# A non-local block in f32: theta and phi by plain f32 matmuls of 64 columns on two column tiles, theta's stack filled by transfers

## The reference

```python
theta = einsum('bhwc,cd->bhwd', x, W_theta)             # 32 channels, 1024 pixels
phi   = maxpool2x2(einsum('bhwc,cd->bhwd', x, W_phi))   # 32 channels, 256 cells
g     = maxpool2x2(einsum('bhwc,cd->bhwd', x, W_g))     # 128 channels, 256 cells
beta  = softmax(einsum('bqd,bkd->bqk', theta, phi), axis=-1)
tmp   = einsum('bqk,bkv->bqv', beta, g)
out   = gamma * einsum('bhwv,vc->bhwc', tmp, W_o) + x
```

## Time and profile before

| | |
|---|---|
| median of 2 runs | 240.32 us (240.01 and 240.63) |
| span of the profiled execution, first to last instruction | 237.7 us; the page gives no other time of its own for it |
| median less that span | 2.6 us |
| PE busy | 232.0 us, 98% |
| DVE busy | 205.3 us, 86% |
| POOL, ACT busy | 167.3 us (70%), 147.8 us (62%) |
| granted TensorE clock | 0.999 of full |
| moved by transfers | 51.14 MB, 215 GB/s |
| chain that ended last | PE 89%, DMA 5%, DVE 4% |

### The profile page before, as it was taken

The page is one execution under the profiler, slowest core; times in us unless marked ns, Lnnn a source line. Parts: engine busy times, 40 slices in busy tenths (PEclk is TensorE's granted clock), DMA queues, the critical chain, the costliest instruction groups (busy, mean ns, idle before and its releaser), DMA issues.

```text
span 237.7 us, 4361 instructions
## 1 busy us (share of the span) xinstructions
PE 232.0 (98%) x1464; PEld 207.8 (87%) x1464; DVE 205.3 (86%) x475; ACT 147.8 (62%) x274; POOL 167.3 (70%) x119
## 2 busy tenths in 40 slices
PE   7999999999999999999999999999999999999994
PEld 4777888988989899898989989898998989989794
DVE  5699988989888898988989899898988989899785
ACT  3665948577483866838477492847748385645640
POOL 1488698868679686768867677786867868642870
PEclk9999999999999999999999999999999999999999
DMA  7693029396592937739194683928659293725854
GB/s 238 220 365 128 3 70 337 130 272 258 119 374 88 337 151 242 292 105 382 60 327 191 194 341 108 343 85 289 241 150 383 61 338 139 247 107 190 318 204 181
DMA packets 14934, 51.14 MB, mean 215 GB/s; under 512 B 1856, under 2 KB 2496, under 8 KB 14912
## 3 DMA queue, kind: packets, MB, share of 16 engines
q1 hardware_dynamic: 14512, 50.67, 60.6%
q10 hardware_dynamic: 400, 0.20, 0.3%
HBM read 33.95 MB, written 16.78 MB: 213 GB/s over the span
## 4 chain that ended last, share of the span: by engine, by line
PE 89%; DMA 5%; DVE 4%; issue 1%; ACT 1%; SPq 0%; DVEq 0%
PE proj L209 23%; PE out L350 18%; PE proj L216 12%; PE proj L350 8%; PE score L255 6%; PE shift L350 6%; PE shift L310 5%; PE score L350 4%; PE score L282 4%; DMA x_t<-in_xt 2%; DMA out<-y_sb 2%; PE shift L209 1%; DVE y_sb L669 1%; DVE neg_parts L643 1%; PE score L265 1%; PE out L282 1%
## 5 line engine op out<-in xcount | busy, mean ns | idle before, releaser
L564 POOL TENSOR_TENSOR e_lo<-e_sb,e_hi 128x512 fp32r<-128x512 f32 x64 | 82.0, 1294 | 45.7 <-ACT e_sb L488 45.7
L559 POOL TENSOR_TENSOR x_lo<-x_t,x_hi 128x1024 fp32r<-128x1024 f32 x30 | 71.8, 2399 | 8.7 <-ACT x_hi L444 8.7
L485 ACT ACTIVATE e_hi<-shift 128x512 fp32r<-128x512 f32 x60 | 36.0, 600 | 17.9 <-PE shift L310 17.0
L209 PE MATMUL proj<-x_hi,w_hi 128*128 128x512 f32 x118 | 46.8, 397 | 0.1
L209 PE MATMUL proj<-x_hi,w_lo 128*128 128x512 f32 x118 | 46.6, 395 | 0.0
L643 DVE TENSOR_REDUCE neg_parts<-score 128x2 f32<-128x512 f32 x64 | 43.6, 686 | 1.1 <-PE score L255 0.2
L350 PE MATMUL out<-G_lo,e_hi 128*128 128x258 f32 x132 | 37.4, 284 | 0.0
L350 PE MATMUL out<-G_hi,e_hi 128*128 128x258 f32 x132 | 37.4, 283 | 0.0
L216 PE MATMUL proj<-x_lo,w_hi 128*128 128x512 f32 x118 | 37.3, 396 | 0.0
L350 PE MATMUL out<-G_hi,e_lo 128*128 128x258 f32 x132 | 37.2, 282 | 0.0
L488 ACT ACTIVATE e_sb<-shift 128x512 f32<-128x512 f32 x60 | 36.1, 602 | 0.0
(11 more groups left out here) (107 smaller groups left out, 480.8 us busy)
## 6 DMA issues: line engine op xcount, KB each, us to landing
x_t<-in_xt SPq DMA_DIRECT2D x32, 512.0 KB, 5.2
x_n<-in_xn SPq DMA_DIRECT2D x32, 512.0 KB, 7.6
out<-y_sb SPq DMA_DIRECT2D x31, 512.0 KB, 6.2
w_sb<-in_w_proj SPq DMA_DIRECT2D x1, 256.0 KB, 2.8
theta<-neg_hi ACTq DMA_DIRECT2D x16, 4.0 KB
theta<-neg_lo SPq DMA_DIRECT2D x16, 4.0 KB
out<-y_sb SPq DMA_DIRECT2D x1, 256.0 KB, 2.1
wo_sb<-in_w_out SPq DMA_DIRECT2D x1, 128.5 KB, 5.7
```

Source lines behind the costliest of these rows:

```text
L209: nc.tensor.matmul(bank_[:, :], w[:, c, cols:cols + P], x_hi[:, i % 2, h, c, :], start=(c == 0 and n == 0), stop=False)
L485: nc.scalar.activation(e_hi[:, i % 2, n, :], shift_bank(i, n)[:, :], ACT.Exp)
L559: nc.gpsimd.tensor_tensor(x_lo[:, i % 2, h], x_t[:, i % 2, h], x_hi[:, i % 2, h].bitcast(f32), ALU.subtract).then_inc(x_lo_ready, 1)
L564: nc.gpsimd.tensor_tensor(e_lo[:, i % 2, n, :], e_sb[:, n, :], e_hi[:, i % 2, n, :].bitcast(f32), ALU.subtract).then_inc(e_lo_ready, 1)
```

## The change

- `theta_phi` is now one step per image and no longer six f32r matmuls per half. It uses x and the weights as they are, in f32: for each channel chunk, one matmul of 64 columns (W_theta, W_phi) by 512 pixels for each half. Half 0 writes PSUM rows 0 to 63 and half 1 rows 64 to 127 of one bank. It needs neither x_hi nor x_lo.
- Theta now exists once per half. `theta_high` and `theta_low` work on 128 rows (both halves, phi's rows with them) and write new tiles `theta_hi` and `theta_lo`. `theta_into_stack` on SP puts them into the stack: four transfers for hi, two for lo, and one that doubles phi's hi block.
- `phi_pool` is one reduction on 128 rows; `phi_high` and `phi_low` pick phi's rows per half.
- x_t has three slots instead of two; w_hi and w_lo hold W_g alone.
- The order at the head of a stage changes on PE, ACT, DVE and SP.

```diff
-PROJ = P + DV
+TP = 2 * DK
+PROJ = TP + DV
...
-        phi_max = outb[1][THETA:P, 0:NK]
+        phi_max = outb[1][:, 0:P]
+        def tp_bank(i):
+            return proj[0] if i == 1 else proj[1]
...
+            def theta_into_stack(i):
+                sp.wait_ge(theta_hi_ready, i + 1)
+                for h in range(2):
+                    rows, pixels = slice(TP * h, TP * h + DK), slice(HALF * h, HALF * (h + 1))
+                    for r in (0, 2 * DK):
+                        sp.dma_start(theta[r:r + DK, i % 3, pixels].bitcast(f32),
+                                     theta_hi[rows, :].bitcast(f32)).then_inc(theta_in, 16)
+                sp.wait_ge(phi_hi_ready, 2 * i + 2)
+                sp.dma_start(phi[DK:2 * DK, i % 3, :].bitcast(f32),
+                             phi[0:DK, i % 3, :].bitcast(f32)).then_inc(phi_in[i % 2], 16)
+                sp.wait_ge(theta_lo_ready, i + 1)
+                for h in range(2):
+                    rows, pixels = slice(TP * h, TP * h + DK), slice(HALF * h, HALF * (h + 1))
+                    sp.dma_start(theta[DK:2 * DK, i % 3, pixels].bitcast(f32),
+                                 theta_lo[rows, :].bitcast(f32)).then_inc(theta_in, 16)
...
+            def theta_phi(i):
...
+                elif i > 2:
+                    pe.wait_ge(y_ready, TILES * (i - 3) + 4)
+                for c in range(CC):
+                    for h in range(2):
+                        last = nc.tensor.matmul(tp_bank(i)[TP * h:TP * (h + 1), :], w_sb[:, c, 0:TP],
+                                                x_t[:, i % 3, h, c, :], start=(c == 0), stop=(c == CC - 1))
+                last.then_inc(tp_ready, 1)
...
             def values(i, h):
...
-                    pe.wait_ge(theta_lo_ready, 2 * i + h + 1)
-                    pe.wait_ge(phi_pooled, 2 * i + h + 1)
-                project(i, h, P, value_bank(i, h), g_ready)
+                    pe.wait_ge(theta_lo_ready, i + h)
+                    pe.wait_ge(phi_pooled, i + h)
...
             def scores(i, n):
                 if n == 0:
-                    pe.wait_ge(theta_lo_ready, 2 * i + 2)
+                    pe.wait_ge(theta_in, theta_loads(i))
+                    pe.wait_ge(phi_in[i % 2], loads(i))
...
-            def theta_high(i, h):
-                act.wait_ge(tp_ready, 2 * i + h + 1)
-                nc.scalar.copy(theta[0:THETA, i % 3, HALF * h:HALF * (h + 1)],
-                               proj[h][0:THETA, :]).then_inc(theta_hi_ready, 1)
+            def theta_high(i):
+                act.wait_ge(tp_ready, i + 1)
+                if i > 0:
+                    act.wait_ge(theta_in, theta_loads(i - 1))
+                nc.scalar.copy(theta_hi[:, :], tp_bank(i)[:, :]).then_inc(theta_hi_ready, 1)
...
-            def phi_pool(i, h):
-                dve.wait_ge(tp_ready, 2 * i + h + 1)
+            def phi_pool(i):
+                dve.wait_ge(theta_hi_ready, i + 1)
...
-            def theta_low(i, h):
-                rows, pixels = slice(DK, 2 * DK), slice(HALF * h, HALF * (h + 1))
-                dve.wait_ge(theta_hi_ready, 2 * i + h + 1)
-                v.tensor_tensor(theta[rows, i % 3, pixels], proj[h][rows, :], theta[rows, i % 3, pixels].bitcast(f32),
+            def theta_low(i):
+                v.tensor_tensor(theta_lo[:, :], tp_bank(i)[:, :], theta_hi[:, :].bitcast(f32),
                                 ALU.subtract).then_inc(theta_lo_ready, 1)
```

More of the change, by code:

```diff
@@ L91, in nonlocal_block @@
         x0_in = sem("x0_in")
-        xt_in = [[sem(f"xt_in{s}{h}") for h in range(2)] for s in range(2)]
+        xt_in = [[sem(f"xt_in{s}{h}") for h in range(2)] for s in range(3)]
         xn_in = [[sem(f"xn_in{s}{h}") for h in range(2)] for s in range(2)]
@@ L118, in loads_t, with theta_loads @@
         def loads_t(i, h):
-            return loads(i) - 16 if i % 2 == 0 and h == 0 else loads(i)
+            return 16 * (i // 3) if i % 3 == 0 and h == 0 else 16 * (i // 3 + 1)
+        def theta_loads(i):
+            return 6 * 16 * (i + 1)
         def neg_loads(i):
@@ L153, in _ @@
             sp.dma_start(wo_sb[:, :], w_out).then_inc(wo_in, 16)
[L154 to L156 removed]
+            for h in range(2):
+                load_t(1, h)
+            theta_into_stack(0)
+            for h in range(2):
+                load_t(2, h)
             for h in range(2):
                 load_n(0, h)
+            theta_into_stack(1)
             for h in range(2):
@@ L201, in first_project @@
                     w, x = ((w_hi, x_hi), (w_lo, x_hi), (w_hi, x_lo))[n]
-                    last = nc.tensor.matmul(proj[0][:, :], w[:, c, 0:P], x[:, 0, 0, c, :],
+                    last = nc.tensor.matmul(value_bank(0, 0)[:, :], w[:, c, :], x[:, 0, 0, c, :],
                                             start=(n == 0 and c == 0), stop=(n == 2 and c == 0))
[L204 to L227, removed]
+                last.then_inc(g_ready, 1)
             def values(i, h):
@@ L395, in _ @@
                 if s > 2:
[L396 to L402, removed]
+                    scores(b, 0)
+                    theta_phi(a)
+                    shifted(d, 2)
+                    values(a, 0)
+                    scores(b, 1)
+                    shifted(d, 3)
+                    values(a, 1)
+                    scores(b, 2)
+                    scores(b, 3)
                 if a < LAST:
@@ L519, in _ @@
                 if s > 2:
-                    for h in range(2):
-                        theta_high(a, h)
-                        exps(d, 2 + h)
+                    theta_high(a)
+                    exps(d, 2)
                     phi_high(a)
+                    exps(d, 3)
                 if a == 2:
@@ L732, in _ @@
                 if s > 2:
-                    for h in range(2):
-                        phi_pool(a, h)
-                        theta_low(a, h)
-                        maxima(b, h)
+                    maxima(b, 0)
+                    phi_pool(a)
+                    theta_low(a)
+                    maxima(b, 1)
+                    g_pool(a, 0)
                     phi_low(a)
-                    g_pool(a, 0)
                     maxima(b, 2)
```

137 lines of the change are left out of this document (78 added, 59 removed).

## The result

The changed kernel took 244.33 us (244.01 and 244.66) against 240.32: 1.017 times the time before, interval 1.0124 to 1.0216. Run once more beside a fresh series of the kernel before, it took 243.92 against 239.83, 1.018 (1.009 to 1.026). It is slower, by 1.7 to 1.8%, and both intervals reach a little above 2%. The forecast was 239, and its opening 1.5 us late.

The account below looks back on a forecast made before the run. TensorE's queue was taken as the bound: 13 stages at -0.22 us give -2.9, the opening +1.5, so the span goes from 237.7 to 236.3; plus 2.6 makes 239 us. The range for 8 in 10 was 231 to 259.

Parts of the forecast that it names:

- main case: The forecast of 239 us itself, given a chance of 0.40 and its own range of 234 to 246.
- What bounds the kernel: Whole run: TensorE, busy 98% of the span; what leaves its queue leaves the time unless something else becomes too late.
- Price of an f32 matmul: 0.93: theta_phi: one plain f32 matmul of 512 pixels costs 0.93 us, four times 0.234; lower bound 0.47.
- Five steps of pieces, 2.33: theta_phi: eight pieces of four matmuls, partly overlapping across column tiles, take five steps, 2.33 us per image.
- rival 1: theta_phi: column tiles run fully side by side, four matmuls take 1.87 us, time 232.5; chance 0.30.
- Change of tiles, 0.10: TensorE going to 64-column tiles and back: 0.05 us each way, 0.10 per image; upper bound 0.70 for both.
- rival 3: theta_phi: weight loads not hidden add 0.8 us per image, time 250; chance 0.10.
- Wait on proj1, 0.15: `values(a, 1)` waits for `theta_low`: 2.25 us of work against 2.10 of cover, so TensorE waits 0.15 per stage.
- Stages in sum: Each of 13 like stages: -2.80 + 2.33 + 0.10 + 0.15 = -0.22 us, together -2.9.
- The opening, +1.5 (to +4): Images 0 to 2, without slack for the stack: turn of image 1's maxima 1.5 us later; bounds -1 and +4.
- The clock: TensorE's clock was expected to stay full, 2.4 GHz, throughout the changed kernel.
- The transfers in the stages: zero: Seven stack transfers per image have two or three us of slack, cost zero; DMA share rises from 0.69 to about 0.78.

Follow-up runs that it names:

- e5: Changed kernel with theta_phi's loops half by half and, from image 2 on, both halves on one column tile (rows 0 to 63); 268.29 us in one execution.
- e6: Changed kernel with theta_phi's loops half by half and, from image 2 on, each matmul 128 columns wide, writing all 128 rows; 264.50 us in one execution.
- e3: Changed kernel with GpSimd making g_lo ahead of x_lo(a+1, 0) in the like stages; 239.84 us, 1.000 of the kernel before.
- e1: Changed kernel with image 2's x loads ahead of the first stack transfers and image 0's x_n loads behind the second ones; 242.65 us, 1.0111 of the kernel before.
- e7: Changed kernel with only ScalarE's opening order new: theta_hi(0) first, then wo_hi, x_hi(1, 1) and g_hi(0) ahead of theta_hi(1); 243.17 us, 1.0107 of the kernel before.
- e8: Changed kernel with e3's g_lo order, new opening orders on SP, ScalarE and TensorE, and two slots for theta_hi and theta_lo; 233.97 us, 0.976 of the kernel before.
- e12: Changed kernel with g_lo's order of e3 and new opening orders of SP and ScalarE, but one slot and TensorE's order unchanged; 236.56 us, 0.986 of the kernel before.

## Why the prediction was wrong

It forecast 239, within 2% and slightly faster. Its range held the time, its sign did not. (The range of its main case, 234 to 246, does not follow from its terms: -4.2 - 1 and +4.9 + 4 around 240.3 give 235 to 249.) By its own steps:

- **What bounds the kernel.** Right for the stages: a stage became shorter by what left TensorE's queue, less the wait named below.
- **Price of an f32 matmul: 0.93.** Near: two pieces of 0.43, thus 0.86, on one tile and at full width alike (e5, e6).
- **Five steps of pieces, 2.33.** Wrong, rival 1 was right: the tiles run fully side by side, 1.71 + 0.16 = 1.87. The kernel with one tile for both halves shows it by its 3.58. I inferred from "every start is behind the last" that pieces queue singly; no row before had two matmuls on different tiles, so it said nothing on that.
- **Change of tiles, 0.10.** Mis-sized: 0.16 in and 0.20 out, 0.36 in all, absent in the full-width kernel. These rows fit the rule that I weighed there (the Trainium skill, TensorEngine Tiling (Array Packing), Key Properties: a change of tiling mode drains the engine), at half of the upper bound I had given it. They do not fit the rule behind rival 3 (the Trainium skill, TensorE: Matmul & The Clock Gate, Part 3: a weight load overlaps a running matmul only where the row group differs): with both tiles on the same rows, two loads per 0.43 us added nothing to the pitch of the pieces.
- **Wait on proj1, 0.15.** It did not occur. I charged the tail of 0.2 to the chain only; it also holds back the `shift` matmul (0.43), so it is in the cover too. VectorE's chain was as forecast (0.70 and 0.68). It ended at 104.27, and `values(a, 1)`, whose first record starts at 104.44, came in the pitch of the queue, with 0.17 to spare where I had 0.15 missing.
- **A wait that the prediction did not name:** mix, 0.33 us per stage. g_lo stands behind a 2.4 us x_lo and ends 9.94 us after the head of its stage in both kernels (102.63 - 92.69 before, 110.15 - 100.21 now). But in the shorter stage the turn of mix comes 9.97 us after the head and no longer 10.74, and that leaves no room. The kernel e3 removed the wait whole.
- Stages in sum: forecast -0.22, measured -2.80 + 1.87 + 0.20 + 0.33 = -0.40 each. So in the stages the change was better than forecast, and that the two sums lie so near is in part luck: the terms were off by -0.62 (the pieces, 1.71 for 2.33), +0.26 (change of tiles), -0.15 (proj1) and +0.33 (mix).
- **The opening, +1.5 (to +4).** This is the step that failed: measured +9.1. "Scores of image 0 wait for the transfers: copy at about 10.6 us ... landing near 15.5" was right for the copy of image 0 (10.73) and 1.5 us short for the landing (17.05). "Stack 1 lands near 22" was not: 28.34. And the path that I did name, loads of image 2, x_hi(2), g_hi(0) and mix(0) "to about 20.3", came at 25.93 and, run again, 26.21; the turn of image 1's maxima, forecast for 32.6, at 40.57. I had left out four waits in the code that was in front of me: the copy of theta 1 waits until transfers of image 0 have landed (one slot); g_hi(0), and by it g_lo(0), VectorE's g_max and the maxima, stand behind that copy; stack 1 stands behind 2 MB of loads for landing, 6.3 us and not 2; and the small transfer of the maxima too. I had judged "loads land in 7.6 us" harmless for the stack in the stages, where it is, and not used it for the opening. With the single fixes (e1, e7) the time fell by 1.3 us at most, and the next wait stood beside the one removed; the orders together with g_lo's gave 236.56, and with two slots and TensorE's order 233.97.
- **The clock** was granted at 0.50 of full (1.2 GHz) from 24 to 30 us, after TensorE had been busy 1.73 of the 6 us before; the forecast had it full throughout.
- **The transfers in the stages: zero.** Right for TensorE: no chain of a middle stage of the changed kernel holds one, with the DMA share at 0.78 as forecast. (The chain of e8 does hold one stage transfer, neg_lo's at 194.51, 3.40 us.) **The end** was priced at nothing and cost 0.8 us. There the stack of image 15 has no stage of slack either, and TensorE waits 1.25 us for it (218.80); that this wait is the 0.8 us is not shown.
- VectorE at 11.52 of 14 us, forecast 11.4: right.

That the opening, and not the stages, holds the loss is shown, by the account (+9.1 against -4.9 and +0.8) and by the new opening: it brings the head of stage 3 to 37.92 and, at the same order in the stages, the time from 239.84 (e3) to 233.97. How its gain is divided is shown only in part: 3.3 us came with the orders of SP and ScalarE (e12 against e3, on two chips), 2.6 with slots, TensorE's order and ScalarE's further change (e8 against e12), and the spread of the opening, up to 2.5 us, is as large as these steps.

## What to carry to other kernels

A step moved from an engine's own write to transfers is free only where there is slack between its landing and its use, here most of a stage; the first and last passes of the pipeline have no such slack, so walk them with every wait of the new code, slots included, and keep bulk loads behind small urgent transfers in the queue. Price a new opening by the latest of all its paths, not by the one that comes to mind first. And when a fix of one wait gains little, look for the one beside it before giving it up; a second profile of the same kernel can show it, as its chain may end on the other path.

## What the runs showed of the hardware

- A plain f32 matmul is two matmul records, each with its weight load, 0.43 us apart for 512 columns at the full clock, whether 64 or 128 columns wide: 0.86 us, against 0.234 us for an f32r matmul.
- Two such matmuls on different column tiles run side by side, in either program order (chunk by chunk or half by half): 1.87 and 1.88 us for four instead of 3.58 on one tile.
- Going from full width to 64-column tiles and back cost 0.16 + 0.20 us; f32 at full width among f32r cost 0.02.
- The first matmul behind a wait brought 0.2 us more for its group in the chain: 0.94 instead of 0.72 at mix behind a wait of 0.12, 0.33 instead of 0.11 for the turn of the maxima, 0.72 instead of 0.47 for two shifts (23.62 in e8).
- Issues of the 64 KB transfers within SBUF took 0.59 us each on SP. They landed in 2.0 us with no load issued just ahead of them, and in up to 6.3 us behind 2 MB of loads; with those loads moved behind them they landed in 2.0 again (e1).
